# Exps of 128x1536 over two slots of three PSUM banks, with a constant scale, in a softmax attention

## The reference

```python
x = inputs.reshape(B, T, NUM_HEADS, HEAD_DIM).transpose(0, 2, 1, 3)
q = x * rotation_params[None, :, None, :]
k = x * entangle_params[None, :, None, :]
v = x
attn_scores = jnp.einsum('bhid,bhjd->bhij', q, k) * scale      # 64 heads of 2048 x 2048
attn_weights = jax.nn.softmax(attn_scores, axis=-1)
out = jnp.einsum('bhij,bhjd->bhid', attn_weights, v)
```

## Time and profile before

| what | value |
|---|---|
| time, median of 3 runs (lowest, highest) | 3663.8 us (3662.5, 3665.08) |
| the profiled execution: its time, its span | 3660.84 us, 3658.7 us |
| first exp starts | 80.47 us |
| the later layers' first instruction | 2144.87 us |
| busy share over the span: PE, DVE, ACT, POOL | 83%, 41%, 70%, 6% |

### The profile page before, as it was taken

One profiled execution on the slowest core, in us unless ns is written; L12 is line 12 of the kernel. 1 busy time (PEld: TensorE's weight loads), 2 busy tenths in 40 slices (PEclk: granted clock), 3 DMA queues, 4 the chain that ended last, 5 costly groups with the idle time before them and its releaser, 6 DMA issues. The chain is left out here.

```text
span 3658.7 us, 48266 instructions
## 1 busy us (share of the span) xinstructions
PE 3020.7 (83%) x18050; PEld 1239.1 (34%) x18050; DVE 1483.3 (41%) x3473; ACT 2545.0 (70%) x2627; POOL 214.3 (6%) x183
## 2 busy tenths in 40 slices
PE   1888888888888888888888856667888888889996
PEld 0211211211111111112111124445566666665664
DVE  5234211211211202211211136656777777766664
ACT  1999999999999999999999952222333333333332
POOL 0000000000000000000000001111111111111110
PEclk9999999999999999999999988788999999999998
DMA  6111101101101101111100012221112111110110
GB/s 200 52 33 35 48 31 37 46 27 39 43 31 43 42 27 45 36 37 43 37 29 27 28 32 63 64 58 47 47 58 68 58 52 52 52 52 30 46 40 18
DMA packets 115950, 169.35 MB, mean 46 GB/s; under 512 B 41360, under 2 KB 90768, under 8 KB 115472
## 3 DMA queue, kind: packets, MB, share of 16 engines
q1 hardware_dynamic: 115728, 166.37, 14.2%
HBM read 107.62 MB, written 58.72 MB: 45 GB/s over the span
## 5 line engine op out<-in xcount | busy, mean ns | idle before, releaser
L371 ACT ACTIVATE probs<-ps,exp_scale 128x1024 f32<-128x1024 f32 x2048 | 2058.6, 1587 | 0.2 <-PE ps L269 0.2
L331 PE MATMUL ps<-probs,vals 128*32 128x512 f32 x8192 | 1091.7, 605 | 0.0
L269 PE MATMUL ps<-qT,kT 64*128 64x512 f16 x4096 | 779.4, 387 | 299.7 <-ACT probs L371 274.4
L269 PEld LDWEIGHTS ps<-qT,kT 64*128 64x128 f16 x4096 | 195.2, 92 | 1409.4 <-ACT probs L371 1276.2
L503 DVE COPY sums<-ps 128x512 f32<-128x512 f32 x64 | 44.3, 692 | 1324.3 <-PE ps L331 1324.3
L331 PEld LDWEIGHTS ps<-probs,vals 128*32 128x32 f32 x8192 | 161.3, 108 | 242.1 <-issue 240.2
L768 PE MATMUL layers_ps<-weight_mem,hT 128*128 128x256 f32 x1024 | 231.8, 386 | 0.0
L762 PE MATMUL layers_ps<-yT,weight_mem 128*128 128x512 f32 x512 | 227.8, 597 | 2.5 <-ACT hT L1001 2.4
L1028 ACT ACTIVATE gate<-layers_ps 128x512 f32<-128x512 f32 x96 | 57.3, 597 | 243.9 <-PE layers_ps L916 198.6
L768 PEld LDWEIGHTS layers_ps<-weight_mem,hT 128*128 128x128 f32 x1024 | 198.0, 195 | 28.8
L916 PE MATMUL layers_ps<-n4T,weight_mem 128*128 128x512 f16 x768 | 178.2, 388 | 31.1 <-DVE n4T L1251 23.4
(11 more groups left out here) (156 smaller groups left out, 2740.2 us busy)
## 6 DMA issues: line engine op xcount, KB each, us to landing
split_dram<-parts SPq DMA_DIRECT2D x32, 512.0 KB, 3.0
qT<-split_dram SPq DMA_DIRECT2D x128, 128.0 KB
kT<-split_dram SPq DMA_DIRECT2D x128, 128.0 KB
xs<-in_x_dram SPq DMA_DIRECT2D x4, 2048.0 KB, 17.2
qT<-split_dram SPq DMA_DIRECT2D x128, 64.0 KB
kT<-split_dram SPq DMA_DIRECT2D x128, 64.0 KB
heads_dram<-result SPq DMA_DIRECT2D x64, 128.0 KB, 7.0
attn<-heads_dram SPq DMA_DIRECT2D x16, 512.0 KB, 5.4
```

What stands on the lines that cost most here:

```text
L269: last = nc.tensor.matmul(SCORES[slot][:, n * BANK:(n + 1) * BANK], kT[buf][rows, j * P:(j + 1) * P], qT[buf][rows, q0:q0 + BANK], start=T ...
L331: mm = nc.tensor.matmul(ACC[32 * c:32 * c + 32, :], vals[buf][:, j, :], probs[:, j % PROBS, c * BANK:(c + 1) * BANK], start=(j == 0), stop ...
L371: nc.scalar.activation(probs[:, j % PROBS, half * T // 2:(half + 1) * T // 2], SCORES[slot_of(at)], ACT.Exp, scale=exp_scale[:, head:head ...
```

## The change

Four things change together.

1. An exp covers three chunks of 512 queries: chunk g = 64 head + 4 j + c, and exp n takes chunks 3n to 3n + 2, across blocks and heads. That makes ceil(4096 / 3) = 1366 exps, the last of one chunk. The six score banks are two slots of three.
2. The scale of the exp is a constant. What it did per head is now in the operands: the square root of the channel's width goes to q (`q_factor`) and the rest to k (`k_factor`). The parts are three per operand (high, low times 2048, high over 2048), so a round stores 6 blocks for 4.
3. `probs` is a ring of 15 chunks (before 16, as 4 blocks of 4).
4. PE issues scores by groups of three chunks. At block j it issues the groups up to two beyond the exps that block j needs, each behind the exp before the last one, then waits for the block's exps, then runs the block's four matmuls. At a head's end nothing further stands ahead of the wait for `sums_ready`.

```diff
-SLOTS = 3
-AHEAD = 3
+CHUNKS = BB * QC
+WIDE = 3
+EXPS = -(-NHD * CHUNKS // WIDE)
+SLOTS = 2
-PARTS = 2
+PARTS = 3
-PROBS = 4
+PROBS = 15
...
+def exps_through(chunks):
+    return -(-chunks // WIDE)
+def chunks_of(n):
+    return range(n * WIDE, min((n + 1) * WIDE, NHD * CHUNKS))
...
+            for dst, src in ((rot_col, rot), (ent_col, ent)):
+                for half in range(KC):
+                    sp.dma_start(dst[:, half:half + 1], src[half * GH:(half + 1) * GH, :].rearrange("h d -> (h d)").unsqueeze(1)).then_inc(rot_loaded, 16)
...
+            pool.wait_ge(setup_step, WIDTH_READY)
+            pool.tensor_tensor(inverse_root[:, :], width[:, :], neghalf[:, 0:KC], ALU.pow).then_inc(root_ready, 1)
...
+            def wide_scores(n):
+                if n >= SLOTS:
+                    pe.wait_ge(exps_done, n - SLOTS + 1)
+                for g in chunks_of(n):
+                    head, j, c = g // CHUNKS, g % CHUNKS // QC, g % QC
+                    if g % CHUNKS == 0:
+                        operands(head, head // GH, head % GH)
+                    rows = slice(COPIES[g % 2], COPIES[g % 2] + STRIP)
+                    last = nc.tensor.matmul(SCORES[n % SLOTS][:, g % WIDE, :], kT[head % 2][rows, j * P:(j + 1) * P],
+                                            qT[head % 2][rows, c * BANK:(c + 1) * BANK], start=True, stop=True)
                 last.then_inc(scores_ready, 1)
...
-                        pe.wait_ge(exps_done, head * HALVES + 2 * j + 2)
+                        at = head * CHUNKS + j * QC
+                        for n in range(exps_through(at) + SLOTS, min(exps_through(at + QC) + SLOTS, EXPS)):
+                            wide_scores(n)
+                        pe.wait_ge(exps_done, exps_through(at + QC))
...
-                        for half in range(2):
-                            i = 2 * (j + AHEAD) + half
...
-                            half_scores(i % HALVES, slot_of(at), buf if i < HALVES else 1 - buf)
...
+            for n in range(EXPS):
+                first, width = chunks_of(n)[0], len(chunks_of(n))
+                if chunks_of(n)[-1] >= PROBS:
+                    act.wait_ge(probs_free, (chunks_of(n)[-1] - PROBS) // QC + 1)
+                act.wait_ge(scores_ready, n + 1)
+                nc.scalar.activation(probs[:, first % PROBS:first % PROBS + width, :], SCORES[n % SLOTS][:, 0:width, :], ACT.Exp,
+                                     scale=OPERAND_SCALE ** -2).then_inc(exps_done, 1)
...
-                factors = (OPERAND_SCALE, k_factor[:, group % KC:group % KC + 1])
-                for i, factor in enumerate(factors):
-                    ins = V.tensor_scalar(out[:, i * PARTS, :], TURN, factor, None, ALU.mult)
-                ch.link(ins)
-                for i, factor in enumerate(factors):
-                    ins = V.scalar_tensor_tensor(out[:, i * PARTS + 1, :], TURN, factor, out[:, i * PARTS, :], ALU.mult, ALU.subtract)
+                for i, factor in enumerate((q_factor, k_factor)):
+                    ins = V.tensor_scalar(qk[:, i, :], TURN, factor[:, group % KC:group % KC + 1], None, ALU.mult)
                 ins.then_inc(round_read, 1)
                 dve.wait_ge(round_read, group * ROUNDS + r + 1)
+                high, low, high_down = out[:, 0:PARTS + 1:PARTS, :], out[:, 1:2 * PARTS:PARTS + 1, :], out[:, 2:PARTS + 2:2, :]
+                ch.link(V.tensor_copy(high, qk[:, :, :]))
+                V.tensor_scalar(high_down, high, 1 / LOW_SCALE, None, ALU.mult)
+                ch.link(V.tensor_tensor(qk[:, :, :], qk[:, :, :], high, ALU.subtract))
+                ch.link(V.tensor_scalar(low, qk[:, :, :], LOW_SCALE, None, ALU.mult))
```

More of the change, by code:

```diff
@@ L22 @@
 GROUPS = NHD // GH
-HALVES = 2 * BB
-SLOTS = 3
-AHEAD = 3
+CHUNKS = BB * QC
+WIDE = 3
+EXPS = -(-NHD * CHUNKS // WIDE)
+SLOTS = 2
 ROUNDS = QC
 ROUND_AT, GENERAL_AT = 4, 8
-PARTS = 2
+PARTS = 3
 STRIP = 64
+PARTS_MAX = 2
 BIAS = 2 * D
@@ L32 @@
 COPIES = (0, STRIP)
-OPERAND_SCALE, MAX_SCALE = 2.0 ** 11, 2.0 ** 15
+OPERAND_SCALE, LOW_SCALE, MAX_SCALE = 2.0 ** 2, 2.0 ** 11, 2.0 ** 15
 TINY = 1e-30
 SAFE = 75.0
-PROBS = 4
+PROBS = 15
 N = 512
@@ L105, in softmax_attention @@
         rot_row, ent_row = sb("rot_row", [P, C]), sb("ent_row", [P, C])
-        head_width, head_inverse, exp_scale = sb("head_width", [P, H]), sb("head_inverse", [P, H]), sb("exp_scale", [P, H])
-        k_factor = sb("k_factor", [P, KC])
+        width, root, inverse_root = sb("width", [P, KC]), sb("root", [P, KC]), sb("inverse_root", [P, KC])
+        rot_col, ent_col = sb("rot_col", [P, KC]), sb("ent_col", [P, KC])
+        q_factor, k_factor = sb("q_factor", [P, KC]), sb("k_factor", [P, KC])
         stats, mv, ve, rstd = sb("stats", [P, BB, 6]), sb("mv", [P, BB, 2]), sb("ve", [P, BB]), sb("rstd", [P, BB])
@@ L112, in softmax_attention @@
         widest_weight = sb("widest_weight", [P, 2])
-        probs = sb("probs", [P, PROBS, T])
+        probs = sb("probs", [P, PROBS, BANK])
         staged = sb("staged", [P, QC, P])
+        qk = sb("qk", [P, 2, BANK])
         parts = [sb(f"parts{i}", [P, 2 * PARTS, BANK], FP16) for i in range(2)]
@@ L127, in softmax_attention @@
         ps = ctx.enter_context(nc.psum_tensor("ps", [P, 8, BANK], F32))
-        SCORES = [ps[:, 2 * s:2 * s + 2, :].rearrange("p a n -> p (a n)") for s in range(SLOTS)]
+        SCORES = [ps[:, WIDE * s:WIDE * (s + 1), :] for s in range(SLOTS)]
         ACC = ps[:, 6, :]
@@ L150, in softmax_attention @@
         MAX_STEPS = 5
-        SPLIT_STEPS = 1
+        SPLIT_STEPS = 3
         LOADS = len(COPIES) * 4 * 16
-        FACTORS_SCALED = 1 + 4 * len(COPIES) + 2 + 1 + 2 + 4
+        WIDTH_READY = 1 + 4 * len(COPIES) + 2 + 3
         block = ctx.enter_context(nc.Block())
@@ L177, in load_operands @@
                 if not (isinstance(head, int) and head < 2):
-                    sp.wait_ge(scores_ready, (head - 1) * HALVES)
+                    sp.wait_ge(scores_ready, exps_through((head - 1) * CHUNKS))
                 src = split_dram[bass.ds(group, 1), :, e * D:(e + 1) * D, :].rearrange("g s p t -> (g s) p t")
                 for at in COPIES:
[L181 to L184, removed]
+                    sp.dma_start(qT[buf][at:at + 2 * D, :], src[0:2]).then_inc(qk_loaded[buf], 16)
+                    sp.dma_start(qT[buf][at + LAST:at + LAST + D, :], src[2:PARTS]).then_inc(qk_loaded[buf], 16)
+                    sp.dma_start(kT[buf][at:at + 2 * D, :], src[PARTS:PARTS + 2]).then_inc(qk_loaded[buf], 16)
+                    sp.dma_start(kT[buf][at + LAST:at + LAST + D, :], src[PARTS + 2:2 * PARTS]).then_inc(qk_loaded[buf], 16)
             def store_result(head, buf):
@@ L302, in operands @@
                 pe.wait_ge(qk_loaded[e % 2], (group * (GH // 2) + e // 2 + 1) * LOADS)
[L304 to L307, removed]
             for r in range(ROUNDS):
@@ L313, in _ @@
             general_scores(0, 0, 0)
[L314 to L318, removed]
+            for n in range(SLOTS):
+                wide_scores(n)
             def group_of_heads(group, last_group):
-                first = group * GH * HALVES
                 for e in range(GH):
@@ L330, in group_of_heads @@
                         for c in range(QC):
-                            mm = nc.tensor.matmul(ACC[32 * c:32 * c + 32, :], vals[buf][:, j, :], probs[:, j % PROBS, c * BANK:(c + 1) * BANK],
+                            mm = nc.tensor.matmul(ACC[32 * c:32 * c + 32, :], vals[buf][:, j, :], probs[:, (at + c) % PROBS, :],
                                                   start=(j == 0), stop=(j == BB - 1), tile_position=(0, 32 * c))
@@ L341, in group_of_heads @@
                             general_scores(nxt, nxt_group, nxt_e)
-                        if j + AHEAD == BB and not last:
-                            operands(nxt, nxt_group, nxt_e)
-                        for half in range(2):
-                            i = 2 * (j + AHEAD) + half
[L346 to L349, removed]
-                            half_scores(i % HALVES, slot_of(at), buf if i < HALVES else 1 - buf)
                     pe.wait_ge(sums_ready, head + 1)
@@ L384, in _ @@
                 setup.done(V.memset(t[:, :, :], 0.0))
-            dve.wait_ge(rot_loaded, 16 * 2)
-            by_head = lambda t: t[:, :].rearrange("p (h d) -> p h d", h=H)
-            setup.link(V.scalar_tensor_tensor(rot_row[:, :], rot_row[:, :], D ** -0.5, ent_row[:, :], ALU.mult, ALU.mult))
+            dve.wait_ge(rot_loaded, 16 * (2 + 2 * KC))
+            setup.link(V.scalar_tensor_tensor(rot_col[:, :], rot_col[:, :], D ** -0.5, ent_col[:, :], ALU.mult, ALU.mult))
+            setup.link(V.scalar_tensor_tensor(width[:, :], rot_col[:, :], -1.0, rot_col[:, :], ALU.mult, ALU.max))
+            setup.link(V.tensor_scalar(width[:, :], width[:, :], TINY, None, ALU.max))
+            assert setup.n == WIDTH_READY
+            setup.done(V.scalar_tensor_tensor(rot_row[:, :], rot_row[:, :], D ** -0.5, ent_row[:, :], ALU.mult, ALU.mult))
```

(14 more changed lines are left out.)

6 lines of the change are left out of this document (3 added, 3 removed).

## The result

| | before | changed |
|---|---|---|
| time, median (lowest to highest) | 3663.2 us (3660.4 to 3665.1) | 3570.6 us (3568.9 to 3572.1) |
| span of the profiled execution | 3658.7 us | 3569.4 us |
| first exp starts | 80.47 us | 86.79 us |
| from the first exp's start to the last one's end | 2058.8 us | 1958.5 us |
| from there to the end | 1519.4 us | 1524.1 us |

The ratio is 0.9748, with a 95% interval of 0.9731 to 0.9765. The change is faster by 2.5%, and 3572 had been forecast.

The account below looks back on a forecast made before the run. The attention was taken as bound by ACT's count of exps times 1.005 us. Terms -205.8 + 89.5 + 14.4 + 10 = -91.9 took 3660.8 to 3568.9; the median, 3.0 above, gave 3572 us, 80% range 3535 to 3653.

Parts of the forecast that it names:

- exps, undisturbed: ACT in the attention: 1365 exps at 1.357 us plus a short last one, 1852.8 us against 2058.6, -205.8 us.
- ends of heads: PE stops at the wait for the sums before the next scores: ACT loses 1.42 us at 63 heads, +89.5 us.
- rounds: Four transposes at j = 4 add 0.59 us to PE; 0.51 reaches ACT, 28 times, +14.4 us.
- elsewhere in the stream: Steady stream of the attention: PE's scores are always ready in time, ACT never waits, 0 us.
- start: first exp later; PE slow: Before the first exp: DVE's longer rounds 7.4 us, larger stores 0.7, slow PE 2 more; +10 us, from 5 to 18.
- later layers: The layers after the attention are bound elsewhere and left alone, as before.
- the 79 ns that I gave to the operand: Per exp on ACT: 1106 ns alone with the scale operand against 1027 with a constant scale.
- the open choice of the prediction: Whether the operand's cost survives in a stream; 1357 ns per exp taken, rival hidden at 1435 ns, 3650 us, 12%.
- 0.08 us to spare: Steady stream: at worst scores are ready 1.28 us into an exp of 1.357, so ACT never waits.
- a head of the first kind: A head's end without PE's extra lag: stall 1.08 us at the wait, then 0.17 twice, together 1.42.
- heads of the others: Heads ending with PE 0.17 or 0.35 us behind: 1.25 or 1.42 lost at the wait, 0.17 or nothing afterwards.

Follow-up runs that it names:

- experiment 2: The kernel before with the changed kernel's operands and constant scale, but its own exps of 1024 columns, slots, ring and PE order: 3491.4 us, ratio 0.9533.
- experiment 1: The changed kernel with the exp's constant scale read from a per-partition operand, so the width alone: 3653.4 us, ratio 0.9973.
- Experiment 3: The changed kernel with the four transposes at a head's end made twice: 3598.9 us.
- 5: The changed kernel with the next head's first group of scores put ahead of the wait for the sums: 3525.6 us, ratio 0.9632.
- experiment 4: The kernel before with the four transposes at a head's end made twice: 3667.7 us, ratio 1.0012.
- 8: The changed kernel with PE's order written out by a plan from measured durations and a ring of 18 chunks of probs: 3489.7 us, ratio 0.9536.
- 9: The kernel before with the constant scale alone, run again beside the planned order with 18 chunks on one chip: 3490.8 us, ratio 0.9536.

## Why the prediction was right, step by step

The span fell by 89.3 us where 91.9 had been summed. The terms, from the starts and ends of all 1366 exps in the trace (what each took over the undisturbed 1.342, summed by its place in the head):

| term | predicted | measured |
|---|---|---|
| exps, undisturbed | 1852.8 us (-205.8) | 1832.3 us (-226.5) |
| ends of heads | +89.5 | +95.3 |
| rounds | +14.4 | +18.6 |
| elsewhere in the stream | 0 | +10.0 |
| start: first exp later; PE slow | +8 and +2 | +6.3 and +2.2 |
| later layers | 0 | +4.7 |

**The exp.** 1357 ns had been taken and 1343 came. Of the 14 ns, 6 are the exp alone (1451 for 1457) and 8 the overlap, 0.108 us where I had carried over 0.10. The 1106 ns that I read as an exp alone in the earlier trace rows is the shortest of its line. The first exp of the earlier trace rows took 6.14 - 5 x 1.005 = 1.115, so the overlap was 0.11 in the kernel before too, and the 79 ns that I gave to the operand are 90: 1.114 for 1.023 alone, in the traces of the kernel before and of experiment 2. That the operand's cost survives in a stream was the open choice of the prediction, and experiments 1 and 2 settle it: 0.09 us for each exp, at 1536 (1.432 against 1.343) and at 1024 columns (1.005 against 0.917). The Trainium skill ("ScalarE: Activation LUTs", What ACT_TABLE_LOAD costs), which the prediction cited, puts a pointer operand at about 93 ns, and these runs agree. Its 186 ns + 0.833 ns per column gives an estimated 1466 ns for one alone, where 1451 was measured, and its overlap of about 93 ns is below the 108 here.

**The steady stream.** I had found 0.08 us to spare and called it thin. With the shorter exp the slip is 0.187 per block and 0.02 is left. In the trace 89 exps away from heads' ends and rounds are 0.08 us late and nine are 0.19 late: +10.0. So the "0 us" of the steady stream was wrong. An exp that waits also loses its overlap, which the walk left out: the price of a wait is its idle time and 0.11 more. The 20 us of the shorter exp went there: 10 in the steady stream, 6 at the heads' ends, 4 in the rounds. The errors cancel, in part because a shorter exp leaves PE less room, in part by luck, and the total is better than its parts.

**The end of a head.** The mechanism and its place held, and its size nearly so: 1.42 each, and 1.51 measured (1.47 to 1.56). Experiment 3 shows that the transposes lie on the path, 5 that moving scores past the wait gives back nearly half. The next scores stood at 2.46 for 2.50, the transposes 0.58 for 0.59, and the wait 1.07 us for 1.08 in a head of the first kind, 1.18 for 1.25 and 1.36 for 1.42 in most heads of the others. What was off is the lost overlap, 0.11 at every wait.

**The rounds.** 0.66 each for 0.51, for the same two reasons: less room on PE, and the lost overlap.

**The start.** DVE's part of a round, in the changed kernel's timeline, for the earlier trace rows:

```profile
38.82 0.75 DVE L425 TENSOR_SCALAR qk<-ps,q_factor 128x512 f32<-128x512 f32 x1 [1.21 <-PE ps L268]
...
40.26 0.69 DVE L429 CAST parts<-qk 128x1024 f16<-128x1024 f32 x1
40.99 0.43 DVE L430 TENSOR_SCALAR parts<-parts 128x1024 f16<-128x1024 f16 x1
41.33 1.22 DVE L431 TENSOR_TENSOR qk<-qk,parts 128x1024 f32<-128x1024 f32 x1
42.59 0.69 DVE L432 TENSOR_SCALAR parts<-qk 128x1024 f16<-128x1024 f32 x1
...
43.42 0.43 DVE L420 COPY staged<-xs 128x512 f32<-128x512 f32 x1
```

4.60 us for the 4.75 worked out: the cast and the last scaling are 0.69 (0.67), the subtraction 1.22, and the scaling from fp16 to fp16 only 0.43. Against 2.88 before this is 1.72, four times 6.9. The stores land in 3.7 us on the page, for 3.0 (0.7 had been taken). The first scores start 7.27 us later (85.75 for 78.48), the first exp only 6.32. ACT's table load of 1.28 us stands between the two in the kernel before and at 0.72 us here; I had not seen that. Experiment 1 has it between them again, and there 2.39 us pass from the first scores to the first exp, for 1.04 in the changed kernel.

**The later layers.** They have no edit in any of these kernels and take 1519.4 us before, 1524.1 in the changed kernel, 1519.4 in experiment 2 and 1523.2 in experiment 4. In the windows view the granted clock of their stretch is 0.92 before and 0.91 after. The eleven traces divide in the same way: 0.92 in the four of 1518 to 1519.4 us, 0.91 in the seven of 1521 us and more. The kernel before has two such levels of its own: its 17 runs beside experiments 1 to 4 are eight from 3659.7 to 3661.0, eight from 3664.3 to 3665.5 and one between, with nothing changed. So the +4.7 cannot be laid to the change, and differences of up to 5 us between two medians can come from here. Whether the clock is the cause, and what decides it, was not tried.

**What the prediction did not ask.** It summed the change as a whole. The four combinations say more: before 3663, width alone 3653, constant scale alone 3491, both 3571. Added to the constant scale, the width makes the kernel slower by 79 us: it takes the 682 overheads of 0.06 us that are left (1878 to 1834 us, 44 us) and gives up three slots, and the scores ahead of the wait, for 124 us of stalls where there were 4. That makes 76 us; the rest lies in the start and the later layers. Even with the planned order and the long ring, the 44 us that the width saves are eaten by 45 us more of late exps (experiments 8 and 9).

## What to carry to other kernels

Where one engine is the bound by its count of instructions, split a change into what makes each instruction cheaper and what makes fewer of them: a per-partition operand of ACT cost 0.09 us per instruction here, more than the 0.06 us of fixed cost that was left afterwards. Walk the order of the feeding engine through its longest interruption, counting how many outputs stand ready ahead of it; wider slots in the same PSUM are fewer slots, and an in-order queue that waits in front of the next feed turns into a stall of the bound engine. A long interruption is passed by interleaving the feed with it. Where the feeder is busy for nearly all of the bound engine's time (here an estimated 28 us of PE in a head of 28.6 us of exps, from the 0.53, 1.00 and 0.59 above), every place in its order counts.

## What the runs showed of the hardware that was not expected

Four more transposes behind four cost 0.44 us where the first four take 0.58 to the next scores. ACT's table load stood at 0.72 us in the changed kernel, whose first exp has one wait ahead of it, but at 85.61 us in experiment 1 and 86.33 in experiment 2, whose first exp has two; that the waits decide it is a reading of the code and was not tested. An exp's overlap with the one before it was 0.106 to 0.109 us in the kernel before, the changed one and experiments 1 and 2, so with an operand or a constant scale and at 1024 or 1536 columns, and an exp that had to wait was longer by that much.
